# Issuing the value products of attention in two groups of three instead of six places

## What is computed

```python
x = x + _L0_conv_ref(_gn(x), ...)      # deformable 3x3 convolution: 9 bilinear samples a pixel
t = _to_tokens(x)                      # 8 x 1024 tokens x 64
t = t + _L1_attn_ref(_ln_t(t), ...)    # 16 heads of 64, rope, causal softmax, output projection
t = t + _L1_ffn_ref(_ln_t(t), ...)     # spectral filters, long convolutions
x = _from_tokens(t, x)
```

```python
att = jnp.einsum('bqhd,bkhd->bhqk', q, k) / jnp.sqrt(jnp.asarray(E, x.dtype))
att = jnp.where(causal, att, jnp.asarray(-jnp.inf, x.dtype))
att = jax.nn.softmax(att, axis=-1)
y = jnp.einsum('bhqk,bkhd->bqhd', att, v).reshape(B, S, H * E)
```

## Time and profile before

| | |
|---|---|
| median of three runs | 3327.86 us |
| lowest, highest | 3325.12, 3328.08 us |
| profiled execution, first to last instruction | 3326.7 us |
| TensorE matmul busy | 3045.5 us, 92% |
| VectorE busy | 2453.9 us, 74% |
| GpSimd busy | 2104.2 us, 63% |
| ScalarE busy | 1414.7 us, 43% |
| mean granted TensorE clock | 0.962 of full |

### The profile page before, as it was taken

One profiled execution on the slowest core, in us unless ns is written; L12 is line 12 of the kernel. 1 busy time (PEld: TensorE's weight loads), 2 busy tenths in 40 slices (PEclk: granted clock), 3 DMA queues, 4 the chain that ended last, 5 costly groups with the idle time before them and its releaser, 6 DMA issues. The chain is left out here.

```text
span 3326.7 us, 68140 instructions
## 1 busy us (share of the span) xinstructions
PE 3045.5 (92%) x19515; PEld 2139.1 (64%) x19515; DVE 2453.9 (74%) x4044; ACT 1414.7 (43%) x2172; POOL 2104.2 (63%) x2602
## 2 busy tenths in 40 slices
PE   3548999999999999999999999999999698999998
PEld 1235666666666666666666666666666577878787
DVE  4557788778877887887788778877877566665666
ACT  1103444444444444444444444444444255555555
POOL 4656787778778777877787787777777582000000
PEclk7659999999999999999999999999999899999999
DMA  6636556556655665565566556657777653434343
GB/s 186 177 105 155 142 147 157 159 139 154 157 151 142 158 162 141 147 157 159 140 154 154 154 141 158 161 140 143 155 156 145 129 165 104 157 101 155 103 161 103
DMA packets 290942, 488.46 MB, mean 147 GB/s; under 512 B 95630, under 2 KB 113438, under 8 KB 290878
## 3 DMA queue, kind: packets, MB, share of 16 engines
q1 hardware_dynamic: 257198, 394.85, 45.6%
q0 software_dynamic: 33680, 92.71, 11.3%
HBM read 258.70 MB, written 23.66 MB: 85 GB/s over the span
## 5 line engine op out<-in xcount | busy, mean ns | idle before, releaser
L1228 ACT ACTIVATE attention_probs<-attention_pss 128x896 f32<-128x896 f32 (+4 forms) x768 | 621.8, 810 | 975.2 <-PE attention_pss L1077 973.0
L1413 POOL DMA_INDIRECT attention_gat<-table,attention_idx x585 | 556.9, 952 | 191.5 <-issue 96.0
L1161 PE MATMUL attention_psY<-attention_probs,attention_xt 128*64 128x128 f32 (+7 forms) x4386 | 658.1, 408 | 6.2 <-DMA attention_xt<-xt 3.2
L1285 DVE TENSOR_REDUCE attention_mx<-attention_pss 128x2 f32<-128x1024 f32 (+3 forms) x520 | 511.9, 1014 | 36.4 <-PE attention_pss L1090 35.8
L1077 PE MATMUL attention_pss<-attention_QA,attention_KA 128*128 128x512 f32 (+4 forms) x1536 | 509.4, 389 | 30.8 <-DVE attention_mx L1285 17.1
L1764 DVE SCALAR_TENSOR_TENSOR spectral_eo<-spectral_psE,kept_sig,spectral_eo 64x512 fp32r<-64x512 f32 x512 | 384.0, 750 | 187.3 <-ACT spectral_eo L1740 180.8
L1658 PE MATMUL spectral_psE<-spectral_tz,spectral_up 128*128 128x512 f32 (+1 forms) x2304 | 469.3, 362 | 17.1 <-DVE spectral_eo L1764 9.6
L1386 POOL TENSOR_TENSOR attention_nat_l<-attention_qk,attention_nat_h 128x512 fp32r<-128x512 f32 x260 | 404.1, 1555 | 97.9 <-ACT attention_nat_h L1247 97.9
L1740 ACT ACTIVATE spectral_eo<-spectral_psE,kept_sig 64x512 fp32r<-64x512 f32 x512 | 349.9, 683 | 242.2 <-PE spectral_psE L1658 236.9
L1658 PEld LDWEIGHTS spectral_psE<-spectral_tz,spectral_up 128*128 128x128 f32 x2304 | 390.6, 191 | 93.5 <-DVE spectral_eo L1764 14.2
L1077 PE MATMUL attention_pss<-attention_QB,attention_KB 128*128 128x512 f32 (+4 forms) x1536 | 436.8, 342 | 0.0
(11 more groups left out here) (202 smaller groups left out, 3555.8 us busy)
## 6 DMA issues: line engine op xcount, KB each, us to landing
attention_QA<-attention_nat_h SPq DMA_DIRECT2D x520, 128.0 KB
spectral_tz<-phis SPq DMA_DIRECT2D x128, 320.5 KB, 4.7
spectral_tz<-phis SPq DMA_DIRECT2D x128, 320.0 KB, 4.3
attention_xb<-xn SPq DMA_DIRECT2D x66, 512.0 KB, 3.5
attention_wt<-wsplit SPq DMA_DIRECT2D x66, 512.0 KB, 4.3
attention_KA<-attention_nat_h SPq DMA_DIRECT2D x260, 128.0 KB
attention_KB<-attention_nat_h SPq DMA_DIRECT2D x260, 128.0 KB
attention_KA<-attention_nat_l SPq DMA_DIRECT2D x260, 128.0 KB
```

Of the source, the lines that this page charges most:

```text
L1161: ins = pe.matmul(psY[C * half:C * half + C, c0:c1], xt[:, kt_, :], probs[:, q + c0:q + c1], start=first, stop=(j == NS - 1), skip_group_c ...
L1228: act.activation(probs[:, pstep[j]:pstep[j] + width], pss[:, slot, lead:lead + width], ACT.Exp, scale=float(E) ** -0.5).then_inc(s_act, 1)
L1285: ins = dve.tensor_reduce(mx_far[:, :, i - 4] if k0 else mx[:, :, i], scores, AX.X, ALU.max)
L1413: pool.indirect_dma_start(gat[:, n, :, :].rearrange("p q c -> p (q c)"), None, d.table.rearrange("r q c -> r (q c)"), bass.IndirectOffsetO ...
```

## The change

`PV_AT` gets a tuple of products for each of two places, and `PV_LAG` becomes 3: products 3, 4 and 5 of the last head are issued one behind the other behind S1, and products 0, 1 and 2 of the running head behind S4. `pv` itself, the waits in it and all lists of the other engines stay as they are. Ahead of the loop three products are issued instead of four, behind it three instead of two.

```diff
-PV_LAG = 2
+PV_LAG = 3
 KQ_COPIES = 16 * (2 * 6 + 2 * 4)
 
 
-PV_AT = {(0, "end"): -2, (1, "after"): -1, (3, "before"): 0, (4, "before"): 1, (4, "after"): 2, (5, "before"): 3}
+PV_AT = {(1, "after"): (-3, -2, -1), (4, "after"): (0, 1, 2)}
...
                     h, j, _ = ORDER[n]
-                    if (j, place) in PV_AT:
-                        step = PV_AT[j, place]
+                    for step in PV_AT.get((j, place), ()):
                         pv(it, h - (step < 0), step % NS, b)
```

## The result

| | before | after |
|---|---|---|
| median of the timed runs | 3327.97 us | 3542.68 us |
| lowest, highest | 3325.12, 3328.22 | 3534.41, 3543.55 |
| span of the profiled execution | 3326.7 us | 3541.0 us |
| mean granted TensorE clock | 0.962 | 0.922 |

The change makes the kernel slower by 6.4%: ratio 1.0637, 95% interval 1.0623 to 1.0651. I had forecast slower, but 3364 us, with 3381 as the upper end. The kernel lost six times what I said.

What follows compares the result with a forecast made beforehand. PE looked like the bound but already waits on DVE, hiding its 94 us saving; POOL's lateness counts: 32 x (0.74 + 0.46 + 0.10) - 6 = +36 us, giving 3364 us. Range 3308 to 3381, the forecast's own 3355 to 3379.

Steps and rivals of the forecast that it cites:

- PE's savings: Attention stage, per pair of heads: seven joins at 0.15 us and two at 0.21 save 1.47 us, 94 us over 64 pairs.
- The rival that PE is the bound: Whole kernel: all 94 us of PE savings and the 6 us of small gains reach the time, 3228 us; chance 0.03.
- longer than its joins say: Group B (products 0 to 2 behind S4): up to 0.2 us a pair longer, +13 us; counted within the forecast's 0.47.
- S1 to max e: Odd head: S1 starts 0.42 us earlier, but 0.67 + 2.09 us stand behind it, so max e starts 0.77 later.
- The pair's end: Read of odd head's out to next dX shrinks from 1.73 to 1.04 us; POOL 0.69 or 0.74 later against dX.
- The end of m1: DVE's second multiply, ahead of rope 2's read: ends 4.07 us behind add 0, so +0.74 and +0.46 in the two pairs.
- The clock: Attention stage: TensorE taken at full clock throughout its 2313 us; no term for a fall in clock.
- Both additions first: POOL's two additions run before m0; m1 ends 4.30 us behind add 0 in all pairs: 15 us more, 3379; chance 0.12.
- multiply first: m0 issued before add 0; m0 and m1 take 3.10 us: -16 us, 3312, chance 0.17; one pair flips, 3335, 0.13.
- POOL's 0.7 us at the edge: Pair's edge: POOL's work comes 0.69 us later against dX (0.74 in the other pair); most of the forecast hangs on it.
- the two small gains: Waits for a new image's tokens save 3.5 us; S0's waits for the row of negated maxima shrink 2.7; together -6.

Runs made afterwards that it cites:

- group B alone: Changed kernel with only products 0, 1, 2 grouped behind S4; 3 before S5, 4 and 5 at their old places, PV_LAG 2: 3548.32 us, ratio 1.0645.
- third gather first: Changed kernel with POOL's third gather issued ahead of the addition of the odd head's out: 3347.68 us, ratio 1.0051.
- something to do in the wait: Changed kernel plus unused matmuls on TensorE (4 or 13 per even head) while it waits ahead of max b: 3430.43 us, a single run.
- POOL's delay alone: Kernel before, TensorE order untouched, GpSimd delayed at the pair's edge by two memsets behind the addition of out: 3653.22 us, a single run.
- group A alone: Changed kernel with only products 3, 4, 5 grouped behind S1; products 0, 1, 2 at their three old places: 3479.06 us, a single run.
- m1 behind rope 2: Changed kernel with multiply m1 moved on VectorE from before the read of rope 2 to behind it: 3368.19 us, a single run.
- gather first, without and with real rows: Changed kernel with the third gather ahead of out's addition: 3347.68 us; the same with real indices in the padding tiles instead of zeros: 3307.21 us.

## Why the prediction was wrong, by its own steps

**PE's savings: right in size, and none of it reached the time.** In the changed kernel, order of time on PE:

```profile
1031.79 2.17 PE L1161 MATMUL attention_psY<-attention_probs,attention_xt 128*64 128x256 f32 x18
1033.89 1.21 PE L1113 MATMUL attention_pss<-attention_xb,attention_wt 128*128 128x512 f32 x4
...
1068.42 2.18 PE L1161 MATMUL attention_psY<-attention_probs,attention_xt 128*64 128x512 f32 x16
1070.53 0.67 PE L1077 MATMUL attention_pss<-attention_QA,attention_KA 128*128 128x448 f32 x2
```

Group A lasts 2.10 us (predicted 2.09), group B 2.11 (2.11). Each join does save 0.15 us. The rival that PE is the bound fell: none of it reached the time. Group B wasn't longer than its joins say.

**S1 to max e: right.** In the changed kernel, on PE:

```profile
1056.49 0.39 PE L1077 MATMUL attention_pss<-attention_QA,attention_KA 128*128 128x256 f32 x1 [0.18 <-DVE attention_mx L1284]
...
1059.26 0.73 PE L1090 MATMUL attention_pss<-attention_nat_h 64*128 64x512 f32 x4
```

That is 2.77 us (0.67 + 2.09 predicted) where it was 1.57.

**The pair's end: nearly right.**

```profile
1069.79 0.69 DVE L1273 TENSOR_TENSOR attention_scaled<-attention_pss,attention_rec 128x512 f32<-128x512 f32 x1
...
1070.67 1.27 POOL L1393 TENSOR_TENSOR kept_T<-kept_T,attention_scaled 128x512 f32 x1 [2.58 <-DVE attention_scaled L1273]
...
1071.44 0.27 PE L1132 MATMUL attention_pss<-kept_ident,attention_xn 128*64 128x128 f32 x1
```

From the read's end to dX it is 0.96 us; predicted 1.04, before 1.73. S5 hardly waits: it starts 0.05 behind that read, where I had 0.13. POOL therefore stands 0.77 later against dX instead of 0.69, and add 0 starts at 4.98 and 4.89; predicted 4.88 and 4.85.

**The end of m1: the first step that failed.** I took "add 0's start + 4.07, or 4.30" from 62 pairs and let it run on to a distance between add 0 and m0 that none of them had, 0.09 and 0.23 us, where they had 0.54 and more. The two numbers were not a spread with 4.30 as its end; they were two orders in which the engines took turns, and there were more. The long kind gave 5.78 (5.28 to 5.87 us for the two multiplies in the pairs shown), with m1 behind the mask's second instruction and lower 0. The short kind gave 4.05 in 6 pairs, 4.28 to 4.54 in the other 20; these 20 cost 37.38 - 36.40 = 0.98 us each at full clock against my 0.84. The long kind cost 2.16 at full clock against 0.56. This alone makes the waiting 79 us where I had 42.

The rule I had set beside this term, the Trainium skill's SBUF — State Buffer, Who interferes with whom, that DVE and GpSimd hold a shared port in turn, agrees with the times: m0, 1.09 us by itself, took 3.35 and ended 0.8 behind the second addition. That issue order decides doesn't cover what is seen: in the changed kernel m0 started at 1033.02, add 0 at 1033.03, and m0 ended behind both additions. And with add 0 ahead by 0.50 us both additions went first, by 0.57 and 0.97 m0 got in between the earlier trace rows, by 0.73 to 0.80 both additions went first again. The distance doesn't fix m1's turn either: with add 0 ahead by some 0.2 us m1 ended 4.3 to 4.5 behind it in the short kind of the changed kernel, and 5.8 where POOL alone was delayed. What decides it stays open; no run took it apart.

**The clock: the second, and no case at all.** I read the stage's full clock as a given and priced waits by their length. I had written that max b's waits would grow from some tenths to over 1 us a pair, and didn't ask what the clock does behind such a wait. It costs more than the wait: by the estimate above 126 of the 204 us, and no less than 102 of the 214. This step would have failed without the other. From my own terms (m1's end 0.46 and 0.74 later, TensorE 0.7 to 1.0 sooner, 0.35 and 0 of idle before) max b would have been idle for some 1.4 to 1.8 us, and in the short kind of group B alone, idle 1.4 to 1.7, the clock fell in 19 of 26 pairs. The runs show it at full clock again in nearly all pairs with the same groups (third gather first, up to pair 52), and in all with the same late multiplies (something to do in the wait); low with the order of before (POOL's delay alone).

**The rivals.** "Both additions first" came nearest in its mechanism, but I gave it the one price that I had seen, 4.30. The condition of "multiply first" did come about, m0 starting 0.01 us ahead of add 0 in the pair shown, which I had also named as a sign of being wrong; what I had tied to it did not, as both additions still went first. What I wrote as the hinge, that most of the forecast hangs on POOL's 0.7 us at the edge, held: delaying POOL alone gives the loss, and giving the time back takes nearly all of it away. Of the two small gains one came and one did not: the waits for tokens are gone from the table, but the ten waits for `QB` grew from 7.8 to 11.7 us where I had them shrink by 2.7.

## What to carry to other kernels

When a change moves an engine that shares something with another, look at what the time depends on at the new distance, and if the trace has no pair at that distance, put the range at the case where the one waits for all that the other has queued, not at the longest case seen. Price a new idle time of TensorE twice: by its length, and by the half clock behind it, here 1.5 to 4.3 us a pair where it fell, for an idle time of 0.8 to 3.5. A saving on an engine that already waits in each period is worth nothing: it lengthens the wait, and it shifts that engine against all others, and that is what has to be costed.

## What the runs showed of the hardware that I had not expected

The granted clock of TensorE falls to 1.2 GHz in a stage where it is busy 97% of the time at full clock before the change, behind one idle time, for 3.4 to 10.2 us. How often, by the idle time at max b, pairs 0 to 52:

| idle at max b | kernel, kind of pair | clock fell in |
|---|---|---|
| 3.3 to 3.5 us | changed kernel, long; group B alone, long | 54 of 54 |
| 1.8 to 2.5 us | POOL's delay alone, both kinds | 51 of 53 |
| 1.8 to 2.0 us | group A alone, long | 22 of 27 |
| 1.4 to 1.7 us | group B alone, short | 19 of 26 |
| 0.9 to 1.2 us | changed kernel, short | 14 of 20 |
| 1.0 to 1.1 us | m1 behind rope 2, long | 7 of 27 |
| 0.76 us | gather first, without and with real rows, long | 8 of 54 |
| 0.3 us | changed kernel, short | 0 of 6 |

The length of the idle time alone doesn't decide it; what else does is not shown. The Trainium skill, TensorE: Matmul & The Clock Gate, HAM oscillation — how this bites in real kernels, describes such a fall in a kernel whose waits are longer. That a single idle time of about 1 us is enough at times is what these traces add.

Besides:

- Two DVE multiplies of 1.09 us each can take from 3.05 to 5.87 us, by the turns that GpSimd's two additions, mask and subtraction take with them. With a shift of 0.3 us of GpSimd it went from 3.5 to 5.3 (group B alone, long kind).
- Indirect gathers in which all partitions read one table row take three times the DMA time of spread ones: 30.2% against 9.2% of the engines for 5.90 MB in 200 us. TensorE waited up to 4.1 us at a time for another transfer meanwhile, and with spread rows in the same gathers these waits were gone.
